# A projection of field pairs: the second tile's x by a gather, weights in two equal halves, five rows gathered apart

## What is computed

```python
PAIRS = np.array(list(combinations(range(NUM_FIELDS), 2)), dtype=np.int32)   # NUM_FIELDS = 32
xi = x[:, pi, :]
xj = x[:, pj, :]
proj = jnp.einsum('bpd,pod->bpo', xi, W)
return proj * xj
```

## Time and profile before

| what | value |
|---|---|
| median of 3 runs | 670.13 us (670.03 to 671.5) |
| the profiled execution | 671.65 us, its span 669.8 us |
| TensorE, VectorE, ScalarE, GpSimd busy | 87%, 61%, 35%, 62% |
| moved by DMA | 285.15 MB, mean 426 GB/s |
| mean granted TensorE clock | 0.949 |

### The profile page before, as it was taken

One profiled execution on the slowest core, in us unless ns is written; L12 is line 12 of the kernel. 1 busy time (PEld: TensorE's weight loads), 2 busy tenths in 40 slices (PEclk: granted clock), 3 DMA queues, 4 the chain that ended last, 5 costly groups with the idle time before them and its releaser, 6 DMA issues.

```text
span 669.8 us, 7465 instructions
## 1 busy us (share of the span) xinstructions
PE 582.2 (87%) x2704; PEld 341.1 (51%) x2704; DVE 410.3 (61%) x528; ACT 232.7 (35%) x301; POOL 418.6 (62%) x256
## 2 busy tenths in 40 slices
PE   5999989979899798979989898998989979799840
PEld 4565555545555464545545454554545546455520
DVE  0776666737676565765856566566666747576640
ACT  2334334333433334343243433334334243432310
POOL 0867857566685666656585764866757566666630
PEclk9999989979999899999999899898989989999875
DMA  8999999999999999999999999999999999999996
GB/s 345 394 431 439 436 431 418 435 438 431 431 430 439 439 425 431 431 430 443 435 427 429 432 433 426 428 437 430 430 434 424 432 438 433 429 444 420 426 450 296
DMA packets 11337, 285.15 MB, mean 426 GB/s; under 512 B 1792, under 2 KB 1920, under 8 KB 2752
## 3 DMA queue, kind: packets, MB, share of 16 engines
q1 hardware_dynamic: 8576, 270.27, 94.0%
q0 software_dynamic: 2464, 14.68, 5.2%
q10 hardware_dynamic: 288, 0.08, 0.1%
HBM read 25.44 MB, written 260.05 MB: 426 GB/s over the span
## 4 chain that ended last, share of the span: by engine, by line
DMA 54%; PE 22%; POOL 8%; DVE 7%; issue 3%; ACT 2%; SPq 0%; DVEq 0%; ACTq 0%; POOLq 0%
DMA out_dram<-staged 38%; PE proj L355 19%; DMA x_in<-x_dram,rows_sb 16%; POOL staged L279 7%; DVE staged L404 7%; PE proj L333 3%; ACT staged L321 2%; DMA ident_sb<-ident_dram 1%; PE proj L377 1%; POOL x_in L252 0%; POOL x_in L261 0%; ACT x_t L306 0%; SPq L224 0%; DVEq L401 0%; ACT x_sb L299 0%
## 5 line engine op out<-in xcount | busy, mean ns | idle before, releaser
L355 PE MATMUL proj<-w_sb,x_t 64*128 64x512 f32 (+7 forms) x2432 | 543.0, 546 | 35.6 <-ACT staged L321 20.0
L404 DVE TENSOR_TENSOR staged<-proj,x_sb 128x1024 f32<-128x1024 f32 (+7 forms) x528 | 410.3, 827 | 234.9 <-PE proj L355 198.7
L279 POOL TENSOR_TENSOR staged<-staged,x_sb 128x1024 f32<-128x1024 f32 (+4 forms) x224 | 390.4, 1756 | 219.4 <-ACT staged L321 214.8
L355 PEld LDWEIGHTS proj<-w_sb,x_t 64*128 64x128 f32 x2432 | 306.6, 192 | 257.9 <-issue 135.6
L321 ACT ACTIVATE staged<-proj 128x1024 f32<-128x1024 f32 (+4 forms) x224 | 171.5, 785 | 330.4 <-PE proj L355 254.6
L333 PE MATMUL proj<-ident_sb,x_sb 128*128 128x128 f32 x256 | 39.2, 303 | 19.8 <-DVE staged L404 19.8
L333 PEld LDWEIGHTS proj<-ident_sb,x_sb 128*128 128x128 f32 x256 | 31.3, 154 | 38.3 <-DVE staged L404 30.6
L299 ACT ACTIVATE x_sb<-x_in 128x2048 f32<-128x2048 f32 x14 | 26.7, 1910 | 61.8 <-DMA x_in<-x_dram,rows_sb 61.8
L306 ACT ACTIVATE x_t<-proj 128x512 f32<-128x512 f32 (+1 forms) x62 | 35.0, 609 | 14.9 <-PE proj L333 14.9
L261 POOL DMA_INDIRECT x_in<-x_dram,rows_sb x14 | 14.5, 1036 | 2.1 <-issue 0.8
L252 POOL DMA_INDIRECT x_in<-x_dram,rows_sb x14 | 13.5, 964 | 2.6 <-issue 2.6
## 6 DMA issues: line engine op xcount, KB each, us to landing
out_dram<-staged SPq DMA_DIRECT2D x16, 5504.0 KB, 24.8
out_dram<-staged SPq DMA_DIRECT2D x15, 5472.0 KB, 25.8
out_dram<-staged SPq DMA_DIRECT2D x16, 4896.0 KB, 25.3
out_dram<-staged SPq DMA_DIRECT2D x1, 3520.0 KB, 19.3
w_sb<-w_dram SPq DMA_DIRECT2D x1, 2688.0 KB, 21.2
out_dram<-staged SPq DMA_DIRECT2D x1, 1952.0 KB, 14.2
w_sb<-w_dram SPq DMA_DIRECT2D x1, 1664.0 KB, 11.7
w_sb<-w_dram SPq DMA_DIRECT2D x1, 1408.0 KB, 14.5
```

The source lines that it names most:

```text
L279: last = nc.gpsimd.tensor_tensor(product, product, x_sb[tile.parity][:, j * dim:(j + n) * dim], ALU.mult)
L355: last = nc.tensor.matmul(proj[b][h][:, at:at + width], x_t[half, i // 2, :], w_sb[half, col:col + width], start=True, stop=True)
L404: last = nc.vector.tensor_tensor(staged_part(item, i, j, n), proj[b][h][:, at:at + n * dim], x_sb[tile.parity][:, j * dim:(j + n) * dim], ...
```

## The change

Three things are edited. (1) Tile 1's x is no longer loaded by SyncE: GpSimd waits for the row numbers (`rows_sb`), then issues the small and the large gather of tile 1 ahead of its first product, and ScalarE copies `x_in` before step 5 of tile 0 (`FIRST_MOVE_BEFORE`). TensorE's transposes of tile 1 and the small gather of tile 2 wait for that copy. (2) First fields from 16 on change halves (`half_of`), so that both halves have 15,872 columns; the last piece of W then has 128 partitions and 5,888 columns instead of 5,376, and the piece of 64 partitions is gone. The transposes of the high fields read x one field earlier, so that each field lands in the half of its weights. (3) `APART` is rows 15 to 19 instead of 16 to 19.

```diff
 MOVE_BEFORE = 3
+FIRST_MOVE_BEFORE = 5
 APART_BEFORE = 6
 GATHER_BEFORE = 13
...
-APART = range(16, 20)
+APART = range(15, 20)
...
+def half_of(i, fields):
+    return (i + (i >= fields // 2)) % 2
+
+def turned_at(i, fields):
+    return (i + (i >= fields // 2)) // 2
...
-    w_cuts = [0, BANK] + [ends[s] for s in (0, 1, 3, 7, 11)] + [w_ends[1], w_ends[0]]
+    w_cuts = [0, BANK] + [ends[s] for s in (0, 1, 3, 7, 11)] + [w_end]
...
-            for c in range(1, len(w_cuts) - 2):
+            for c in range(1, len(w_cuts) - 1):
                 sp.dma_start(w_sb[:, w_cuts[c]:w_cuts[c + 1]], w[:, w_cuts[c]:w_cuts[c + 1]]
                              ).then_inc(w_loaded[c], 16)
-
-            c = len(w_cuts) - 2
-            sp.dma_start(w_sb[0:dim, w_cuts[c]:w_cuts[c + 1]], w[0:dim, w_cuts[c]:w_cuts[c + 1]]
-                         ).then_inc(w_loaded[c], 16)
-            sp.dma_start(x_sb[1][:], x[P:2 * P, :]).then_inc(x_second_loaded, 16)
...
             def load_apart(number):
-                if number > 2:
-                    pool.wait_ge(x_moved, number - 2)
+                if number > 1:
+                    pool.wait_ge(x_moved, number - 1)
...
             def load_x(number):
-                pool.wait_ge(x_apart_loaded, 16 * (number - 1))
+                pool.wait_ge(x_apart_loaded, 16 * number)
...
+            pool.wait_ge(rows_loaded, 16)
+            load_apart(1)
+            load_x(1)
             every_tile(emit)
...
-                    if item == MOVE_BEFORE and not tile.first and not tile.last:
+                    if item == (FIRST_MOVE_BEFORE if tile.first else MOVE_BEFORE) and not tile.last:
                         move_x(tile)
...
-                        if item == "turn_low" and tile.first:
-                            pe.wait_ge(x_second_loaded, 16)
-                        elif item == "turn_low":
-                            pe.wait_ge(x_moved, tile.number)
+                        if item == "turn_low":
+                            pe.wait_ge(x_moved, tile.number + 1)
```

More of the change, by code:

```diff
@@ L66, in w_columns @@
     for i in range(fields - 1):
-        at[i] = ends[i % 2]
-        ends[i % 2] += (fields - 1 - i) * dim
-    return at, ends
+        h = half_of(i, fields)
+        at[i] = ends[h]
+        ends[h] += (fields - 1 - i) * dim
+    assert ends[0] == ends[1]
+    return at, ends[0]
 def place(segments, dim):
@@ L94, in field_pair_project @@
     steps, groups = plan(fields, dim)
-    w_at, w_ends = w_columns(fields, dim)
+    w_at, w_end = w_columns(fields, dim)
     assert 2 * dim == P and fields == 32 and tiles % 2 == 0 and tiles >= 4
@@ L134, in stores_of @@
         return sum(slot_of[these[0]] == k for these in merged)
-    ends = {s: max(w_at[i] + (j - i - 1 + n) * dim for i, j, n in steps[s][0]) for s in range(len(steps))}
-    w_cuts = [0, BANK] + [ends[s] for s in (0, 1, 3, 7, 11)] + [w_ends[1], w_ends[0]]
+    ends = {s: max(w_at[i] + (j - i - 1 + n) * dim for unit in steps[s] for i, j, n in unit)
+            for s in range(len(steps))}
+    w_cuts = [0, BANK] + [ends[s] for s in (0, 1, 3, 7, 11)] + [w_end]
     assert w_cuts == sorted(set(w_cuts))
@@ L163, in sem @@
             return ctx.enter_context(nc.semaphore(name))
-        w_sb = sb("w_sb", [P, w_ends[0]])
+        w_sb = sb("w_sb", [P, w_end])
         x_in = sb("x_in", [P, fields * dim])
@@ L182, in field_pair_project @@
         x_first_loaded = [sem(f"x_first_loaded{h}") for h in range(2)]
-        x_second_loaded = sem("x_second_loaded")
         x_loaded = sem("x_loaded")
@@ L267, in emit @@
                     if item == APART_BEFORE and tile.number + 2 < tiles:
-                        if tile.first:
-                            pool.wait_ge(rows_loaded, 16)
                         load_apart(tile.number + 2)
@@ L292, in move_x @@
             def move_x(tile):
[L294 to L298, removed]
+                if not tile.first:
+                    _, b, use = list(items(Tile(tile.number - 1, 1 - tile.parity,
+                                                tile.half - 1 + tile.parity)))[-1]
+                    act.wait_ge(emptied[b][1], use + 1)
+                    act.wait_ge(pool_scaled[group_of[pool_steps[-1]]], tile.number)
+                act.wait_ge(x_loaded, 16 * (tile.number + 1))
                 nc.scalar.activation(x_sb[1 - tile.parity][:], x_in[:], ACT.Copy).then_inc(x_moved, 1)
@@ L332, in turn @@
                     k = low + h * (count // 2) + n
+                    at = 2 * k * dim if k < fields // 4 else (2 * k - 1) * dim
                     last = nc.tensor.transpose(proj[b][h][:, n * P:(n + 1) * P],
-                                               x_sb[of][:, k * P:(k + 1) * P], ident_sb[:])
+                                               x_sb[of][:, at:at + P], ident_sb[:])
                 last.then_inc(filled[b][h], 1)
@@ L352, in project @@
                         pe.wait_ge(emptied[b][h], use)
-                    half = slice(h * dim, (h + 1) * dim)
                     for i, col, at, width in pieces(steps[s][h]):
+                        half = slice(half_of(i, fields) * dim, (half_of(i, fields) + 1) * dim)
                         last = nc.tensor.matmul(
-                            proj[b][h][:, at:at + width], x_t[half, i // 2, :],
+                            proj[b][h][:, at:at + width], x_t[half, turned_at(i, fields), :],
                             w_sb[half, col:col + width], start=True, stop=True)
@@ L423 @@
         first = pair_index(i, i + 1, fields) * dim
-        columns[i % 2].append(w_turned[:, first:first + (fields - 1 - i) * dim])
-    halves = [np.concatenate(c, axis=1) for c in columns]
-    w = np.zeros((2 * dim, halves[0].shape[1]), np.float32)
-    for h in range(2):
-        w[h * dim:(h + 1) * dim, :halves[h].shape[1]] = halves[h]
+        columns[half_of(i, fields)].append(w_turned[:, first:first + (fields - 1 - i) * dim])
+    w = np.concatenate([np.concatenate(c, axis=1) for c in columns], axis=0)
     numbers = np.arange(batch, dtype=np.uint32).reshape(-1, P).T
```

## The result

The changed kernel takes 675.71 us (median of 6 runs, 674.39 to 681.43); the kernel before took 670.1 us in the same comparison (6 runs, 669.63 to 671.5). The ratio is 1.0098 (95% interval 1.0082 to 1.0113): slower, by 5.6 us between the medians (6.6 by the ratio). The forecast was 668.9 us with a range up to 670.8. What came is the case of rival D, the late gather, to which I had given a chance of 0.08.

A forecast was written before the change was run, and what follows sets the result against it. The prediction took the DMA stream, with its holes and late last engines, as the bound. Weights -1.5, late store 3 +1.0 and five rows apart -0.7 gave -1.2 us: 670.13 to 668.9 us, range 667.3 to 670.8.

The forecast's parts named there:

- rival D: Tile 1's gather lands late, at 32.9 us; store 3 at 46.8, a hole of 7.4 us; 675.3 us, chance 0.08.
- The bound: DMA stream: its start, the slowest engine's bytes and every hole; it runs dry before store 3 at 40.4 to 41.4 us.
- Weights, -1.5 us: At 24 to 27 us, equal halves remove the half-rate stretch of the 64-partition W piece: -1.5 us on every engine.
- x of tile 1: Gather on GpSimd's queue lands at 26.3 us, the copy ends at 28.3, store 3 slides 1.6 us to 40.2.
- The hole, +1.0 us: Before store 3's first packet at 41.2 us the DMA stream runs dry for 0 to 0.8 us; taken as +1.0.
- Five rows apart, -0.7 us: At the kernel's end, a fifth row off the large gathers relieves the last DMA engine: -1.0 + 0.3 = -0.7 us.
- Rival B: At the end another DMA engine is last, so the rows apart cost 0.3 us; 669.9 us, chance 0.23.

The follow-up runs named there:

- e1_halves: The kernel before with only the weights' part of the change (two equal halves); 669.47 us, ratio 0.9989.
- e2_halves_five: The change without its part on x (tile 1's x again from SyncE behind the weights); 669.27 us, ratio 0.9997.
- e4_busy: The change plus 24 transposes on TensorE that nobody reads, where it waits for ScalarE in tile 0; 675.43 us, ratio 1.0094.
- e6_late1: e2_halves_five plus one GpSimd product into an unread buffer ahead of step 6's product in tile 0; 671.72 us, ratio 1.0019.
- e7_four: The change with four rows apart (16 to 19) instead of five; 676.67 us, ratio 1.0099.
- e8_again: The change itself, unaltered, measured and profiled a second time; 675.0 us, ratio 1.0074 against the kernel before.
- e5_late3: e2_halves_five plus three GpSimd products into an unread buffer ahead of step 6's product in tile 0; 676.41 us, ratio 1.009.
- e3_whole: The change, but tile 1's x by one gather of 128 rows, without the small one ahead of it; 669.31 us, ratio 0.9994.
- e9_later: The change with tile 0's copy and tile 2's small gather moved before step 12, its large gather before step 18; 675.84 us, ratio 1.0087.

## Why the prediction was wrong

**The bound** was right: the stream of stores, with its margin at store 3. The trace of the kernel with five extra products dates its end at 40.2 us, against 40.4 to 41.4 in the forecast.

**Weights, -1.5 us**: right in the stretch it was read from (207 to 408 GB/s), too large in the time. e1_halves measures -0.7 with an interval from -1.4 to 0; e2_halves_five and its repetition, which have the fifth row apart as well, -0.2 and +0.1. Why less arrives at the end is only argued: the kernel ends with its last engine, not with the mean of all.

**x of tile 1: the step that failed.** The forecast put the landing at 26.3 us, and then a rigid slide of 1.6 us to store 3. Measured were 30.5 and 29.6 for the landing, and 8.3 and 6.6 for the slide. Taken apart, with the second profile:

- When the large gather is issued: 15.81 us for the 12.8 of the forecast, 3.0 us. The row numbers land 0.3 us later (5.6 us for 5.3), and the small gather takes 7.2 us for the shortest landing of the earlier trace rows, 6.3: 0.9. The larger part, 1.8 us, I had put at nothing without a reason: GpSimd starts the small gather 1.0 us after the row numbers have landed (6.8 to 7.79) and the large one 0.8 us after the small one has (15.0 to 15.81). The first profile has 1.0 and 0.8 as well.
- From there to the landing: 29.65 - 15.81 = 13.8 us for 13.5. The working with rows and packets held in this profile; in the first it took 15.4.
- The copy's end to tile 2's small gather: 0.9 us in both profiles, for none in the forecast. It is the third handover to GpSimd of the same length.
- From that gather to store 3: 45.23 - 32.46 = 12.8 us, before 38.63 - 26.56 = 12.1. These 0.7 us are the gap in GpSimd's products behind TensorE's stop (0.76 us); e4_busy, where the clock stays up, has none. In the first profile they are 1.5.

In sum 3.0 + 0.3 + 0.9 + 0.7 = 4.9, and with the 1.6 forecast the slide is 6.5, for 6.6 measured. The largest part, 2.7 us, are the three handovers to GpSimd that the forecast had at nothing; the transfers were 1.5 us longer than forecast, and the stop of TensorE added 0.7. The bound that I had written beside the 26.3 (34.6 at the upper end) held the truth, but the chances did not: rival D was said to decide from a landing after 27.6 us, only 1.3 above my value in a range of 24 to 34.6. A chance of 0.08 did not follow from those numbers.

That rival D's 675.3 us stands so near the 675.7 measured is luck. It has the landing at 32.9 us, and it came at 29.6 and 30.5; it takes 2.2 us off for weights and rows, of which little or nothing arrived; and it prices a hole at its own length, which was too cheap. By the forecast's own prices a landing at 29.6 us gives only some 672.1, its edge of 0.3%. These errors cancel.

The Trainium skill (DMA: Bandwidth & Descriptors, section Anatomy of one DMA) gives a GpSimd DMA about 2.0 us plus its bytes at 436 GB/s; for the five rows of 8 KB that would be an estimated 2.1 us. The trace disagrees for a small gather among loads: the two landed 6.6 and 7.2 us after the start of their issue.

**The hole, +1.0 us.** At a store 3 of 40.2 us the line through the experiments gives about +1 to 2 (e6_late1, at 41.22, has +2.5 by the medians, +1.5 by the ratios). So the step from store to time was too cheap as well, and the stream has no spare time beyond the 38.4 to 39.5 us at which the kernels without a hole issue it.

**Five rows apart, -0.7 us**: not seen. The pairs that differ by it stand 0.2 us apart (e1_halves and e2_halves_five, where by the ratios the kernel with five is 0.5 slower) and 1.0 to 1.7 apart (the change's two medians and e7_four, whose intervals overlap). Rival B, that another late engine ends the kernel, fits as well, and is not shown either.

**What stays open** is why a late store 3 costs more than the bytes missing in its hole: with three extra products 7.1 us by the medians and 6.2 by the ratios against 4.3, and in e8_again 4.9 us over the kernel before against (441 - 97) / 441 x 5 = 3.9. The two sides are also not of one execution, since the hole of e5_late3 is read in its slowest one. Within a profile the loss can be split. If the shares of all windows from 660 us on are added up, the mean DMA engine of e2_halves_five is done at 663.5 us and that of e5_late3 at 669.6, 6.1 us later, while the span is 9.7 us longer (676.8 against 667.1). So of these 9.7 us 4.3 are the hole, 1.8 are lost between hole and end, and 3.6 are a tail in which few engines still work (share 0.32 from 668 to 670 us, 0.05 from 674 to 676; in the first profile of the change 0.36 from 672 to 674 and 0.09 from 676 to 678). The middle part need not come from the hole: from 350 to 600 us e5_late3 moves 429 GB/s and e2_halves_five 431, worth 1.2 us, but e3_whole, which has no hole, moves 429 too. In e8_again the mean engine is done 6.6 us later and the span is 7.5 longer, a tail of 0.9; the first profile of the change has 9.1 and 12.5. What makes the tail, and whether the hole does, no experiment here shows.

## What to carry to other kernels

- In a chain of serial DMAs, count from the start of each issue to the start of the next, and add the handover: from a landing (or a copy's end) to the start of GpSimd's next DMA it was 0.8 to 1.0 us here, three times in one chain. Take middle durations for all but one link. The handovers at nothing and the best cases gave 4 us of an error, where 1.3 decided the sign.
- A load that is moved off the critical queue brings its waiters along. List who waits on it (here ScalarE's copy, then GpSimd, and TensorE through the PSUM buffers), put the first of them behind the latest likely landing, and then do the same for the next transfer that the same edit makes late: e9_later repaired tile 0 and broke tile 1.
- Where stores bound a kernel, date the moment at which the stream runs dry without the late store. A product into an unused buffer, once or several times, moves the store by hand and shows slope and margin in four kernels.

## What the runs showed of the hardware

- A gather's landing depends on what streams beside it. A large one took 21.6 us among 44 KB store packets (44.02 to 65.67, e9_later), 13.8 to 15.4 among the loads behind a small one, 11.5 where it was issued at 7.55 us (e3_whole), and 5.8 in the hole of e5_late3 (issued at 42.07):

```profile
DMA to landing us min/median/max: 5.8/5.8/5.8
```

  The Trainium skill (DMA: Bandwidth & Descriptors, section Queues, rings and completion order) says that each DMA engine takes turns between the queues it has work for, a packet at a time; by that rule the size of the neighbour's packets sets the wait, and these figures agree.
- GpSimd does not start its next DMA at once when what it waits for is there: 1.0 us after the row numbers had landed, 0.8 after the small gather had, 0.9 after ScalarE's copy, the same in both profiles of the change. ScalarE's copy starts at the landing (15.10 + 15.4 = 30.5, copy at 30.54).
- TensorE's granted clock read its lower level (0.50, which is 1.2 GHz) from 30 to 35 us and 0.55 from 35 to 40, with a stop of 6.51 us that ended at 33.41. With one of 4.08 us that ended at 32.52 it read 0.75 and 0.91 in the same stretches, and 0.50 from 33 to 35: the same lower level, for a shorter time. With 24 transposes in the stop it stayed at 1.00.
- DMA share and rate can part: in e6_late1 the share from 40 to 45 us is 1.00 at 348 GB/s. In that window its queue of gathers (q0) has 62.1% for 0.95 MB, that of e2_halves_five 35.6% for 0.75 MB:

```profile
q0 software_dynamic: 133, 0.95, 62.1%
```

```profile
q0 software_dynamic: 98, 0.75, 35.6%
```

  So a row of 8 KB took 0.43 us there for 0.31 (share x 5 us x 16 / rows of 8 KB). A hole that is filled by a gather shows in the GB/s more than in the share.
